# A macaron layer on one core: a shorter path to the first routing, more buffers for the weights' split, and the last chunk's end in two halves

## The reference, cut to what matters

```python
def ffn(x):                       # E = 64 experts, F = 64 hidden, D = 128
    shared = silu(x @ Ws_up) @ Ws_down
    aff = x @ centroids.T
    biased = aff + expert_biases
    _, idx = top_k(biased, 8)
    w = sigmoid(take_along_axis(aff, idx))
    w = w / (sum(w) + 1e-08)
    cw = zeros((T, E)).at[rows, idx].add(w)
    h = silu(einsum('td,edf->etf', x, W_up))
    y = einsum('etf,efd->etd', h, W_down)
    return shared + einsum('etd,te->td', y, cw)

def attn(x):                      # q = x Wq, k = x Wk, v = x Wv
    score = softmax(q @ k.T) * NORM_FACT
    return score @ v

x = x + 0.5 * ffn(layernorm(x))
x = x + attn(layernorm(x))
x = x + 0.5 * ffn(layernorm(x))
```

## Time and profile before

| what | value |
|---|---|
| median of 3 runs | 583.32 us (581.55 to 583.37) |
| the profiled execution: its own time, its span | 583.93 us, 582.1 us |
| busy: TensorE, its weight load | 546.1 us (94%), 441.7 us |
| busy: VectorE, ScalarE, GpSimd | 437.9 (75%), 406.2 (70%), 280.7 us (48%) |
| DMA | 73.25 MB, mean 126 GB/s |
| TensorE clock granted, mean | 0.986 of full |

### The profile page before, as it was taken

One profiled execution on the slowest core, in us unless ns is written; L12 is line 12 of the kernel. 1 busy time (PEld: TensorE's weight loads), 2 busy tenths in 40 slices (PEclk: granted clock), 3 DMA queues, 4 the chain that ended last, 5 costly groups with the idle time before them and its releaser, 6 DMA issues.

```text
span 582.1 us, 8666 instructions
## 1 busy us (share of the span) xinstructions
PE 546.1 (94%) x2715; PEld 441.7 (76%) x2715; DVE 437.9 (75%) x913; ACT 406.2 (70%) x800; POOL 280.7 (48%) x248
## 2 busy tenths in 40 slices
PE   3489999899989999989999999899999999999996
PEld 2368777687867777669999999768777777877884
DVE  3778769977996686577777988788768968875663
ACT  4558776686768777476666666677776787687774
POOL 4478765666576567300000000055664766566563
PEclk9689999999999999999999999999999999999999
DMA  6465564455536645000000000046664555666562
GB/s 187 135 199 179 172 193 144 131 176 181 161 125 188 178 155 162 1 1 1 2 0 2 1 2 1 1 139 185 182 193 152 161 198 142 178 175 196 180 191 82
DMA packets 47837, 73.25 MB, mean 126 GB/s; under 512 B 8944, under 2 KB 13488, under 8 KB 47792
## 3 DMA queue, kind: packets, MB, share of 16 engines
q1 hardware_dynamic: 47792, 72.71, 41.0%
HBM read 70.58 MB, written 2.10 MB: 125 GB/s over the span
## 4 chain that ended last, share of the span: by engine, by line
PE 76%; DVE 12%; ACT 3%; POOL 3%; issue 3%; DMA 2%; SPq 1%; POOLq 0%; DVEq 0%; ACTq 0%
PE lrow L874 11%; PE lrow L875 11%; PE lrow L876 11%; PE bank L914 9%; PE bank L916 8%; PE bank L915 8%; PE bank L920 6%; PE bank L1069 3%; PE bank L1071 3%; PE bank L1070 3%; DVE rs L613 2%; DVE gated L588 2%; POOL gpart_lo L249 2%; DVE rs L611 1%; PE bank L875 1%
## 5 line engine op out<-in xcount | busy, mean ns | idle before, releaser
L249 POOL TENSOR_TENSOR gpart_lo<-gated,gpart_hi 128x512 fp32r<-128x512 f32 x176 | 226.6, 1293 | 192.5 <-ACT gpart_hi L410 188.4
L399 ACT ACTIVATE lrow<-lrow 128x512 f32<-128x512 f32 (+1 forms) x256 | 149.7, 585 | 62.0 <-PE lrow L876 61.7
L588 DVE TENSOR_TENSOR gated<-lrow,wide 128x512 f32<-128x512 f32 x170 | 116.5, 685 | 48.4 <-ACT lrow L399 43.7
L410 ACT CAST gpart_hi<-gated 128x512 fp32r<-128x512 f32 x176 | 107.9, 613 | 8.0 <-DVE gated L588 7.3
L914 PE MATMUL bank<-gpart_lo,wdn_hi 128*128 128x512 f32 x256 | 102.2, 399 | 1.6 <-POOL gpart_lo L249 1.4
L916 PE MATMUL bank<-gpart_hi,wdn_hi 128*128 128x512 f32 x256 | 101.6, 397 | 0.0
L915 PE MATMUL bank<-gpart_hi,wdn_lo 128*128 128x512 f32 x256 | 101.1, 395 | 0.0
L588 DVE TENSOR_TENSOR lrow<-lrow,wide 128x512 f32<-128x512 f32 x78 | 54.0, 693 | 30.8 <-ACT lrow L399 30.8
L410 ACT CAST gpart_hi<-lrow 128x512 fp32r<-128x512 f32 (+1 forms) x88 | 52.0, 591 | 30.8 <-DVE lrow L588 30.7
L810 DVE TENSOR_TENSOR pT_lo<-bank,pT_hi 128x512 fp32r<-128x512 f32 x64 | 43.6, 683 | 25.8 <-ACT pT_hi L532 25.8
L249 DVE TENSOR_TENSOR gpart_lo<-lrow,gpart_hi 128x512 fp32r<-128x512 f32 (+1 forms) x88 | 59.9, 680 | 1.3 <-ACT gpart_hi L410 0.6
(11 more groups left out here) (181 smaller groups left out, 989.6 us busy)
## 6 DMA issues: line engine op xcount, KB each, us to landing
wide<-gates_dram SPq DMA_DIRECT2D x496, 128.0 KB, 3.0
raw<-in_w_up SPq DMA_DIRECT2D x8, 256.0 KB, 3.9
raw<-in_w_down SPq DMA_DIRECT2D x8, 256.0 KB, 4.2
x<-in_x SPq DMA_DIRECT2D x4, 256.0 KB, 4.3
gates_dram<-gates SPq DMA_DIRECT2D x8, 128.0 KB, 2.3
out_dram<-x SPq DMA_DIRECT2D x4, 256.0 KB, 3.2
raws<-in_wv SPq DMA_DIRECT2D x1, 64.0 KB, 2.2
raws<-in_wq SPq DMA_DIRECT2D x1, 64.0 KB, 2.1
```

What stands on the lines that cost most here:

```text
L249: return eng.tensor_tensor(gpart[1][0:m, U % NGP, :], gated_at(U)[0:m, :], gpart[0][0:m, U % NGP, :].bitcast(F32), ALU.subtract)
L399: nc.scalar.activation(dst[0:m, :], hid[U % NH][0:m, :], ACT.Silu).then_inc(s_silu, 1)
L410: nc.scalar.copy(gpart[0][0:m, U % NGP, :], gated_at(U)[0:m, :]).then_inc(s_ghi, 1)
L588: nc.vector.tensor_tensor(gated_at(U), a, b, ALU.mult).then_inc(s_gated, 1)
```

## The change

Five things are changed; three constants go with them.

- **First routing.** `x` of chunk 0 comes in two halves, one issued by SP and one by ScalarE; 1/sqrt of the variance is a Sqrt on ScalarE and a reciprocal on VectorE; the turned rows are split in two halves; sigmoid is taken straight from the product with the centroids; the steps that guard a division (`rec`, `aff`) go; the narrow float32r part `rest` is made for the EARLY units only. Wv, Ws_down, the biases, Wq and Wk are issued by GpSimd. TensorE runs matmuls of the identity (`stay_awake`) at the start and between the steps.
- **Weights.** NR = 14 buffers in memory that only attention uses, PRE = 6; ScalarE takes pieces 0 to 2 ahead of the sigmoid, and 3 to 5 behind the gates.
- **Order.** Four up products (LEADS[0]) go ahead of the first gates; unit 0 is split ahead of unit 1; EARLY = 6; `turn_weights` stands at unit 12 and `qk_weights` at unit 15 of chunk 0, with their ScalarE copies at units 13 and 16 and VectorE subtractions at 14 and 17.
- **Unit 32 of chunks 3 and 7** has its low part on VectorE.
- **End.** The last chunk's result is halved, turned, added and stored in two halves; the second is stored by ScalarE.

```diff
-EARLY = 4
+EARLY = 6
-PRE = 8
-LEAD = 2
+PRE = 6
+FIRST = 8
+LEADS = (4, 2)
+WARM = 5
-    NR = 4
+    NR = 14
-        def on_pool(u):
-            return u % 3 != 0
+        def on_pool(U):
+            n, u = divmod(U, UNITS)
+            return u % 3 != 0 and (u < UNITS - 1 or n % NCH < NCH - 1)
...
-            load_x(0)
-            for src, lo, n in ((cent_d, 0, E), (wsup_d, E, F), (wv_d, E + F, D),
-                               (wq_d, LOADED, D), (wk_d, LOADED + D, D)):
+            sp.dma_start(x[:, 0:2, :], x_v[:, 0:2, :]).then_inc(s_x[0], 16)
+            for src, lo, n in ((cent_d, 0, E), (wsup_d, E, F)):
                 sp.dma_start(raws[:, lo:lo + n], src).then_inc(s_small, 16)
-            sp.dma_start(rawd[:, :], wsdn_d).then_inc(s_small, 16)
-            sp.dma_start(bias[:, :], bias_d.partition_broadcast(P)).then_inc(s_bias, 16)
...
+            for dst, src in ((raws[:, E + F:LOADED], wv_d), (rawd[:, :], wsdn_d)):
+                nc.gpsimd.dma_start(dst, src).then_inc(s_value, 16)
+            nc.gpsimd.dma_start(bias[:, :], bias_d.partition_broadcast(P)).then_inc(s_bias, 16)
+            for i, src in enumerate((wq_d, wk_d)):
+                nc.gpsimd.dma_start(raw_qk[:, i * D:(i + 1) * D], src).then_inc(s_qk, 16)
...
+            act.dma_start(x[:, 2:TPC, :], x_v[:, 2:TPC, :]).then_inc(s_x0b, 16)
...
+            nc.scalar.activation(rs[:, 0, 0, :], mv[:, 0, :, 1], ACT.Sqrt, bias=eps[:, 0:1]).then_inc(p_rs, 1)
+            nc.scalar.activation(eps[:, 2:3], eps[:, 0:1], ACT.Sigmoid)
...
+                            first_hi(0)
+                            first_hi(1)
                             piece_hi(0)
-                            pro_hi(n)
-                            for k in range(1, 6):
-                                piece_hi(k)
-                            pro_sil(n)
+                            piece_hi(1)
+                            piece_hi(2)
+                            act.wait_ge(f_bias, 1)
+                            nc.scalar.activation(flat(sil), bank[0][:, 0:TPC * E], ACT.Sigmoid).then_inc(p_sil, 1)
+                            nc.scalar.activation(eps[:, 3:4], eps[:, 0:1], ACT.Silu)
...
+                            make_sel()
+                            silu_unit(0, n)
+                            silu_unit(1, n)
+                            hi_unit(0, n)
+                            silu_unit(2, n)
+                            pro_cwT(n)
+                            silu_unit(3, n)
+                            for k in range(3, PRE):
                                 piece_hi(k)
...
+            def first_top():
+                b = biased[0]
+                dve.wait_ge(s_bias, 16)
+                dve.wait_ge(p_aff, 1)
+                nc.vector.tensor_tensor(b[:, :, :], bank[0][:, 0:TPC * E].rearrange("p (t e) -> p t e", e=E),
+                                        bc(bias[:, :]), ALU.add).then_inc(f_bias, 1)
...
+            def first_chosen():
...
+                nc.vector.scalar_tensor_tensor(out=rec[:, :, :], in0=rest[:, :, :], scalar=LOWEST, in1=sil[:, :, :],
+                                               op0=ALU.is_equal, op1=ALU.mult).then_inc(p_w, 1)
...
+                        first_xT()
+                        stay_awake(1)
+                        first_aff()
+                        for u in range(LEADS[0]):
                             up(u, n)
-                        turn_weights()
+                        stay_awake(2)
                         pro_cw(n)
+                        stay_awake(1)
...
-                        if n == 0 and u == 8:
+                        if n == 0 and u == 12:
+                            turn_weights()
+                        if n == 0 and u == 15:
                             qk_weights()
...
+                    for h in range(2):
+                        half = slice(h * GW, (h + 1) * GW)
+                        nc.scalar.mul(yT[:, half], yacc[1][:, half], 0.5).then_inc(z_y, 1)
+                    act.wait_ge(z_x, 2)
+                    act.dma_start(out_v[:, NT - GT:NT, :], x[:, NT - GT:NT, :]).then_inc(s_out, 16)
```

More of the change, by code:

```diff
@@ L289, in store_gates @@
                 sp.dma_start(gates_d[n], gates[:, :]).then_inc(s_gout, 16)
-            pieces = iter(range(PRE + NR, 2 * WP))
             for n in range(2 * NCH):
@@ L559, in _ @@
                     o_copy(NQ - 1)
-                    for u in range(LEAD):
+                    for u in range(LEADS[1]):
                         silu_unit(u, NCH)
```

224 lines of the change are left out of this document (150 added, 74 removed).

## The result

The changed kernel takes 581.01 us (median of 19 runs, 578.75 to 582.49), the kernel before 583.37 (median of 19 runs beside them, 581.52 to 585.54). The ratio is 0.9943, with a 95% interval of 0.9930 to 0.9956: a gain of 3.3 us, 2.6 to 4.1. Forecast were 7.0, and 573.8 to 580.3 as the range. The profiled execution has a span of 579.4 us (own time 581.23) against 582.1 (583.93). Single executions of either kernel differ by up to 4 us, so the ratios carry the comparison, and steps are read from traces.

The account below looks back on a forecast made before the run. TensorE, busy 546.1 of 582.1 us, was taken as the bound, so only its idle and slow stretches could pay. Terms 5.35 + 0.5 + 0.5 + 0.4 + 0.25 = 7.0 off 583.93 gave 576.9, stated as 576.5; range 573.8 to 580.3.

Parts of the forecast that it names:

- Start of the routing: Chunk 0's first routing: sigmoid can start at 9.6 to 10.9, gates' copy ends at 16.8, 8.5 us earlier.
- the DMAs of GpSimd: Rival, first routing: slow GpSimd DMA issues make the biases late and hold the sigmoid; time 586, chance 0.05.
- The clock for the centroids: First routing: the centroids' product, started at 7.7, ends at 10.5 at the old pace, 9.2 at full clock.
- the first rival: Half clock through the whole first routing: gates near 18.3 instead of 16.8, time 578.0; chance 0.2.
- The port lock: Rival, first routing: VectorE's steps slow beside a late GpSimd, gates 2.5 to 3 us later, time 579.5; chance 0.13.
- From the gates to the restart: Gates to unit 9's up product behind chunk 1's turned rows: 1/sqrt 11.2 us after gates, up product at 34.6.
- The clock at the restart: Chunk 0, up products behind chunk 1's turned rows: if the clock holds, six matmuls run faster; half counted, 0.6 us gained.
- the wait for `turned_lo`: Chunk 0, unit 15: TensorE waits for VectorE's low part of turned Wq and Wk; 1.4 us lost, nothing if VectorE is ahead.
- GpSimd's backlog hides, with 3 us of cover: Chunk 0: unit 17's low part comes 17.1 us after the restart, TensorE wants it after 20.1; no cost.
- the signs of being wrong: Gates ending after 20, VectorE's chain behind `rs` much off 6.4 us, or TensorE waiting for chunk 0's low parts after restart.
- Unit 32, EARLY, the end: Unit 32 at attention 0.5 us, in chunk 7 0.5; early gates nothing; halves at the end 0.4, store 0.25.
- the 0.6: Final sum: the profiled execution lies 0.6 us above the median of the runs, so 576.9 was lowered.

Follow-up runs that it names:

- e12_cold_after: The changed kernel without the identity matmuls of the first routing; 579.78 us, ratio 0.9926 to the kernel before.
- the second profile: The changed kernel itself, run and profiled once more with nothing changed; 580.43 us, ratio 0.9936 to the kernel before.
- e4_relief: The changed kernel with the two products of chunk 1's unnormed weights on VectorE instead of GpSimd; 580.19 us, ratio 0.9924 to the kernel before.
- e3_turned: The changed kernel with VectorE's low part of the turned Wq and Wk ahead of chunk 1's reciprocal; 580.45 us, ratio 0.9914 to the kernel before.

## Why the prediction was wrong

Nearly all of what I forecast is in the traces, but 581.0 lies above the range. The prediction failed in chunk 0 behind the restart, in one wait that it put at nothing and two terms that it added though they cancel, and in treating as fixed what differs from execution to execution.

- **Start of the routing: about 1 us too early.** The gates ended at 17.84 for a forecast 16.8; in five profiles with this start they end between 16.28 and 17.84, mean 17.1. The sigmoid started at 11.93, where the sum had it ready by 9.6 to 10.9; from there ScalarE's queue had no wait and took 5.9 us for 6.4. The cause of the lateness is the rival "the DMAs of GpSimd", in small. I had let the sigmoid stand at 5.6 + 2y, at 8.2 for an issue of y = 1.28; the issue took 0.57, but the landing 7.5 us instead of SP's 3.7, and with this transfer on SP the pieces landed sooner too. Its price is 1.6 us in the traces (0.7 to 2.3) and 3.2 in the times (1.8 to 4.6), where the rival asked for about 10 to reach its 586. By the Trainium skill's DMA: Bandwidth & Descriptors, Anatomy of one DMA (about 2.0 us fixed), it was out; the trace doesn't agree (7.5 us, beside a DMA share of 0.94).
- **The clock for the centroids** was full, which made the first rival wrong, but nothing came of it: without the identity matmuls (e12_cold_after) the time stayed. The port lock didn't reach the gates either: VectorE's last step ahead of the gates' turn ended at 15.41, and ScalarE's queue was the longer one.
- **From the gates to the restart: right.** 17.8 forecast, 17.67 to 17.71 in every profile with this order, before 15.98. The chain behind `rs` took 6.42 for 6.44.
- **The clock at the restart (+0.6) and the wait for `turned_lo` (-1.4): wrong to add them.** The clock was full at the restart in 3 of the 14 profiles of the changed kernel and its variants, and half in the three of the kernel before. In the second profile it brought +1.2 against before, where the first has -0.35. But in the profile with the full clock units 15 to 18 cost 2.9 us, in the other 2.0, for a forecast of 1.75. I priced the wait from TensorE's arrival, but it ends with VectorE, 13.8 to 14.9 us after the restart, so what TensorE gains ahead of it goes into it.
- **"GpSimd's backlog hides, with 3 us of cover": wrong, and with it the largest term missed, 1.1 us.** TensorE waited 0.86 us for a low part at 62.23, one of the signs of being wrong that the prediction named. I counted low parts and pieces at 1.26, not the two products of chunk 1's weights (1.5 us), which stand right ahead of that low part; on VectorE (e4_relief) 1.05 of the 1.1 us came back. GpSimd also waited 2.10 us for ScalarE until 54.21, after TensorE's stand at unit 15; without the stand (e3_turned) that wait was 0.48 and TensorE's was still 0.85, so the stand isn't what makes the backlog.
- **Spells of half clock in chunks 1 and 2** are in no term. They cost 1.0 to 1.2 us each. The first profile of before had none, the one of after had one: of the 2.0 us between the two profiles of the changed kernel, 1.1 are this. Why a rest of the same 1.4 us brings half clock in one execution and not in the next is open.
- **Unit 32, EARLY, the end: right.** 0.5 at attention, about 0 for the six early gates, and 1.15 at the end, for 0.5, 0 and 1.15. The store landed 2.3 us after the last sum in the trace before, not 2.7, which changes no term.
- **A slip:** 576.9 less the 0.6 is 576.3, not 576.5.

In the second profile the start is 0.7 short of the sum (6.0 for 6.7 at the restart), the clock brings 0.6 more, the wait takes 1.1 more and the backlog 1.1: 7.0 becomes 4.7, as measured there. In the first the start is 0.9 short, the clock 0.95, units 12 to 18 about 0.2, and backlog and spell take 1.1 each: 2.7, as measured. The gain of 3.3 us (2.6 to 4.1) lies between them. The kernel before varies as well: its restart, 41.31 in the profile that the sum started from, came at 40.27 and 40.56 in the other two. The three spans before average 582.1, the two after 578.4, which is 3.7 and inside the interval. By the count above, spells cost the changed kernel and its variants 11 / 14 x 1.1 = 0.9 us on average and the kernel before 1 / 3 x 1.1 = 0.4. Three profiles are few, so whether the change makes spells more frequent stays open.

## What to carry to other kernels

A wait of TensorE for another engine's chain costs from TensorE's arrival to that chain's end; what makes TensorE faster ahead of it goes into it as long as that chain doesn't move, so price such waits from the other engine's side and take terms ahead of them together, not added. Before work is moved to where a start path is short, list what small transfers it then hangs on and who issues them: here 32 KB of biases, issued third by GpSimd while the weights stream in, cost 3.2 us (1.8 to 4.6), as much as the whole change had gained. And an idle engine just ahead of its own bottleneck is the first place to look for the next gain: GpSimd stood for 5.55 us ahead of 10 us of queued work, and filling that gap brought 1.95.
